# Quantised block and attention in one block of engine programs, with the first batch's adapter, norm and query/key products between the tiles 21 to 31

## The reference

```python
# 1: quantised block, FF = 1024
scale = cond @ norm_w.T + 1.0
h = x * (scale[:, None, :] * rsqrt(mean(x * x, -1) + 1e-6))
val, gate = split(h @ up_w.T)                  # up_w: [2048, 256]
h = val * gelu(gate)
x = act_quant(h) @ weight_quant(down_w).T + x  # 8-bit rows, ternary weights
# 2: adapter whose weights a generator makes for each batch from cond
Wd_b, Wu_b = Wd + 0.1 * (cond @ Wdd.T + bdd), Wu + 0.1 * (cond @ Wdu.T + bdu)
x = x + relu(x @ Wd_b.T + bd) @ Wu_b.T + bu    # bottleneck of 128
# 3: attention, 16 heads of 16, then a gated feed-forward block
a = gamma * rmsnorm(x) + beta
x = x + alpha * (softmax(q @ k.T / 4) @ v) @ W_o.T
x = x + alpha2 * swiglu(gamma2 * rmsnorm(x) + beta2)
# 4: layer norm with weight, bias and tanh(cond @ lin_w.T + lin_b)
```

## Time and profile before

| | us |
|---|---|
| three executions, median | 1230.28 |
| lowest and highest | 1226.63 and 1235.0 |
| the profiled execution | 1235.64 |
| its span, first to last instruction | 1233.8 |
| PE, DVE, ACT, POOL busy in the span | 1078.5, 720.0, 660.9, 220.4 |
| mean granted TensorE clock | 0.92 |

### The profile page before, as it was taken

One profiled execution on the slowest core, in us unless ns is written; L12 is line 12 of the kernel. 1 busy time (PEld: TensorE's weight loads), 2 busy tenths in 40 slices (PEclk: granted clock), 3 DMA queues, 4 the chain that ended last, 5 costly groups with the idle time before them and its releaser, 6 DMA issues. The chain is left out here.

```text
span 1233.8 us, 16846 instructions
## 1 busy us (share of the span) xinstructions
PE 1078.5 (87%) x5282; PEld 648.6 (53%) x5282; DVE 720.0 (58%) x1166; ACT 660.9 (54%) x890; POOL 220.4 (18%) x261
## 2 busy tenths in 40 slices
PE   4879999995569999999999999998629999999994
PEld 3657777773334434443434343333118777777772
DVE  3756666666145767767776777673035455555553
ACT  4463333333214777877776877665333445554445
POOL 0000000001423244544443444311000000000000
PEclk9889999997665999999999999997669999999997
DMA  9622222230152435354545353531030000000000
GB/s 316 233 74 77 78 77 77 78 105 13 39 141 80 122 94 153 103 138 103 145 100 148 89 157 91 159 67 35 11 120 1 1 17 17 17 17 0 17 18 34
DMA packets 63007, 103.66 MB, mean 84 GB/s; under 512 B 18416, under 2 KB 28144, under 8 KB 61936
## 3 DMA queue, kind: packets, MB, share of 16 engines
q1 hardware_dynamic: 60064, 100.43, 28.0%
q10 hardware_dynamic: 2896, 2.64, 0.9%
HBM read 65.81 MB, written 33.03 MB: 80 GB/s over the span
## 5 line engine op out<-in xcount | busy, mean ns | idle before, releaser
L1099 DVE TENSOR_REDUCE mx<-mx_ps 128x1 f32<-128x512 f32 x512 | 329.9, 685 | 176.4 <-PE mx_ps L1154 176.3
L1154 PE MATMUL mx_ps<-kring,qring 48*128 48x512 f32 x512 | 212.5, 484 | 16.5 <-DVE mx L1099 9.3
L1203 PE MATMUL st_ps<-qring,kring 50*128 50x512 f32 x512 | 195.9, 465 | 14.0 <-ACT shared L1032 10.7
L1203 PEld LDWEIGHTS st_ps<-qring,kring 50*128 50x128 f32 x512 | 81.3, 194 | 171.4 <-issue 108.7
L1032 ACT ACTIVATE pbuf<-st_ps 128x1024 f32<-128x1024 f32 x128 | 129.0, 1022 | 47.1 <-PE st_ps L1203 45.3
L1032 ACT ACTIVATE shared<-st_ps 128x1024 f32<-128x1024 f32 x128 | 128.6, 1023 | 38.8 <-PE st_ps L1203 37.7
L1154 PEld LDWEIGHTS mx_ps<-kring,qring 48*128 48x128 f32 x512 | 90.5, 194 | 56.5 <-DVE mx L1099 47.7
L1375 ACT ACTIVATE p_hi<-shared 128x512 fp32r<-128x512 f32 x64 | 40.4, 631 | 93.6 <-DVE shared L1445 93.6
L1449 DVE TENSOR_TENSOR p_lo<-shared,p_hi 128x512 fp32r<-128x512 f32 x64 | 44.3, 692 | 59.2 <-ACT p_hi L1375 59.2
L479 DVE SCALAR_TENSOR_TENSOR h<-val_ps,r,gelu 128x1024 f32<-128x1024 f32 x32 | 41.1, 1284 | 63.7 <-PE val_ps L563 63.7
L1193 PE MATMUL av_ps<-pbuf,vaug 128*17 128x512 f32 x512 | 71.9, 640 | 3.0 <-ACT oaug L962 2.8
(11 more groups left out here) (215 smaller groups left out, 2160.9 us busy)
## 6 DMA issues: line engine op xcount, KB each, us to landing
chunk<-in_gen_w SPq DMA_DIRECT2D x8, 2048.0 KB, 7.7
qring<-q_parts SPq DMA_DIRECT2D x64, 192.0 KB, 3.5
kring<-k_parts SPq DMA_DIRECT2D x64, 192.0 KB, 4.5
q_parts<-stage SPq DMA_DIRECT2D x16, 512.0 KB, 2.8
k_parts<-stage SPq DMA_DIRECT2D x16, 512.0 KB, 2.8
xres<-in_xT SPq DMA_DIRECT2D x8, 512.0 KB, 10.4
shared<-in_x SPq DMA_DIRECT2D x8, 512.0 KB, 9.8
q_parts<-stage SPq DMA_DIRECT2D x16, 256.0 KB, 3.0
```

What stands on the lines that cost most here:

```text
L1099: nc.vector.tensor_reduce(mx[h // GH % 2][:, col:col + 1], mx_ps[qt % 2][:], AX, ALU.max).then_inc(S["mx_free"], 1)
L1154: nc.tensor.matmul(mx_ps[qt % 2][:], qring[r:r + QROWS, h // GH, h % GH // 2, qt * P:(qt + 1) * P], kring[r:r + QROWS, h // GH, h % GH // ...
L1203: ins = nc.tensor.matmul(st_ps[half][:, kt % 2], kring[r:r + SROWS, g, i % GH // 2, kt * P:(kt + 1) * P], qring[r:r + SROWS, g, i % GH // ...
```

## The change

Blocks 1 and 2 become one function, `quantised_and_attention`, with one list of instructions per engine and no meeting between them. The body of an attention step becomes a function `step(j, ..., i)` on each engine, and `opening` hands out the steps of the iterations -1 and 0 one after another, up to the point that tables by tile name. From iteration 1 on they are looped as before.

- All 32 tiles are written out. The generator makes one round in each of the tiles 2 to 17 (`round_of`), stored by ACT one tile later; SP reads `gen` back once after the last, and DVE adds the base in the tiles 20 to 27. SP loads the attention weights after tile 8's residuals, ACT makes their high parts in tiles 18 and 19, and POOL (before: DVE) the low parts.
- The steps of batch 0 stand in the tiles 21 to 31: adapter down product after down(20) in tile 22, up products at the ends of tiles 22 and 23, mean product in tile 25, query/key products in tiles 27 to 30, stores of the parts by SP as they come. The table of ACT's functions is switched in tile 25 for Ln and Exp and back for the next Gelu.
- After tile 31: down(30), the value products, the transposes of q(31) and x1(30), steps up to (0, 9) with the first head's maxima, down(31), its transposes, then steps up to (0, 15).
- A query/key part goes otherwise from PSUM to `stage`, in every batch: ACT copies the high part straight there, DVE subtracts it from PSUM for the low part, at its place in the step behind the early reductions. The bank is free after that (`qk_lo`). The four products of batch 0 use `misc` too, not the score banks.
- SBUF is laid out by hand: weights and buffers of the opening steps share the place of the generator's chunks, the rings and pbuf share that of the up weights and tile buffers. So the first load of a ring waits for the last value product (`val_done`, NT), and the ones of vaug, the zeros of av_ps and the minus ones in kring are made late: the latter by four DMAs of a row each (`key_units`), queued on SP between ring groups 0 and 1.

```diff
+ACT_PLAN = {21: (-1, 7), 22: (-1, 8), 24: (-1, 11), 25: (-1, 14), 26: (0, 1), 27: (0, 2), 31: (0, 5)}
+DVE_PLAN = {23: (-1, 10), 24: (-1, 11), 28: (0, 2), 29: (0, 3), 30: (0, 4), 31: (0, 5)}
+PE_PLAN = {(22, "gate"): (-1, 8), (22, "val"): (-1, 9), (23, "val"): (-1, 10), (25, "gate"): (-1, 13),
+           (27, "gate"): (0, 1), (28, "val"): (0, 2), (29, "val"): (0, 3), (30, "val"): (0, 4)}
...
+        def opening(step):
+
+            order = [(j, i) for j in (-1, 0) for i in range(NH)]
+            taken = [0]
+
+            def upto(j, i):
+                while taken[0] < len(order) and order[taken[0]] <= (j, i):
+                    step(*flags(order[taken[0]][0]), order[taken[0]][1])
+                    taken[0] += 1
+            return upto
...
+            for cc in range(2, NCHUNK):
+                sp.wait_ge(A["gen_ps"], ROUNDS * (cc - 1))
+                sp.dma_start(chunk[cc % 2][:], gen_w[cc]).then_inc(A[f"chunk{cc % 2}_loaded"], 16)
+                if cc == 4:
+                    sp.wait_ge(A["x1"], 2 * KT)
+                    load_attention_weights(sp)
...
                 if isinstance(b, int) and b == 0:
-                    sp.wait_ge(S["setup"], 2)
+                    sp.wait_ge(A["val_done"], NT)
...
-                        nc.gpsimd.tensor_copy(stage[m % 2][:, 0], tmp[:]).then_inc(S["qk_hi"], 1)
-                        wait_apart(pool, "qk_hi", 4 * p + m + 1, (S["mx_zeroed"], 2))
-                        sub(stage[m % 2][:, 1], tmp[:], stage[m % 2][:, 0].bitcast(F32)).then_inc(S["qk_lo"], 1)
...
-                        copy(tmp[:], qk_bank(j, m)).then_inc(S["qk_f"], 1)
+                    wait(act, f"qk{m % 2}_out", 16 * STORES * (2 * p + m // 2))
+                    copy(stage[m % 2][:, 0], misc[:]).then_inc(S["qk_hi"], 1)
...
+                if 2 <= i < 6 and has_p:
+                    m = i - 2
+
+                    wait(dve, "qk_hi", 4 * p + m + 1)
+                    nc.vector.tensor_tensor(stage[m % 2][:, 1], misc[:], stage[m % 2][:, 0].bitcast(F32),
+                                            ALU.subtract).then_inc(S["qk_lo"], 1)
...
-                            take_misc("qk_f", 4 * p + m + 1)
+                    take_misc("qk_lo", 4 * p + m + 1)
...
+                        if (n, "gate") in PE_PLAN:
+                            upto(*PE_PLAN[n, "gate"])
...
+                        if (n, "val") in PE_PLAN:
+                            upto(*PE_PLAN[n, "val"])
+            down(NT - 2)
+            upto(0, 6)
+            transpose_q(NT - 1)
+            transpose_x1(NT - 2)
+            upto(0, 9)
+            down(NT - 1)
+            transpose_x1(NT - 1)
+            upto(0, NH - 1)
```

1556 lines of the change are left out of this document (789 added, 767 removed).

## The result

| | before | after |
|---|---|---|
| median, same chip (4 runs each), us | 1231.74 | 1188.76 |
| lowest and highest | 1226.63 to 1235.0 | 1181.76 to 1199.82 |
| the profiled execution, its span | 1235.64, 1233.8 | 1181.76, 1180.0 |
| PE, DVE, ACT, POOL busy | 1078.5, 720.0, 660.9, 220.4 | 1058.6, 730.2, 664.8, 165.9 |

The ratio is 0.9643, with a 95% interval from 0.961 to 0.9677: 43 us faster; 34 had been forecast (1196.0, range 1182 to 1214). A second profile of the changed kernel (run r1_after) has a span of 1187.6. Its steps are read beside the first wherever that matters.

What follows compares the result with a forecast made beforehand. TensorE was taken to bound the quantised stage and nearly the attention loop, but not 286 to 400 us. Regular steps 37.6 us earlier, plus 3.5 for the hand-over, gave -34.1 from 1230.3: 1196 us, range 1182 to 1214.

Steps and rivals of the forecast that it cites:

- Moved products: Tiles 21 to 30: batch 0's adapter, mean and query/key products lengthen the tiles by their TensorE time, +10.85 us.
- stalls: Tiles: TensorE waiting on the moved steps' work on other engines, +1.5 us, bounds 0 and 22.
- Rival B: Tiles stall: GpSimd blocks DVE on the shared port, 8 us (1204), or chains cost 22 us (1216); chance 0.2.
- The new tail: From T, the transposes' start after tile 31's value product, to the first maximum product: 13.5 us, between 12.4 and 16.5 (half clock).
- rival A: Clock stays full through tail, maxima and first regular steps, worth 10 us, giving 1186; chance 0.18.
- rival D: After tile 31: ring comes no earlier, waiting for late key parts; up to 10 us more, 1206; chance 0.07.
- Maxima: Before the regular steps: first head and up-adapter product 4.3 us, down(31) with transposes 3.15, six heads 22.6; together 30.0.
- The hand-over: Attention loop: DVE's subtraction after ACT's copy delays the fourth maximum product 0.5 us in each of 7 batches, +3.5 us.
- Rival C: Query/key steps: reductions and maxima stand still 1.9 us in each of 28 steps, loop +53 us, 1246; chance 0.03.
- The sum: Whole kernel: regular steps begin 37.6 us earlier, hand-over adds 3.5, total -34.1 us, median 1196.

Runs made afterwards that it cites:

- r1_after: The changed kernel itself, unmodified, timed and profiled again beside the first group of follow-ups; 1188.51 us, ratio to the kernel before 0.967.
- r1_pool_split: Changed kernel with the old hand-over of query/key parts: ACT copies to tmp, POOL casts and subtracts; 1189.35 us, ratio to before 0.9665.
- r3_end_zero: Changed kernel with av_ps cleared earlier and unused matmuls at the loop's end, two a step in j = 8, up to nine in j = 9; 1178.86 us.
- r2_warm_end: Changed kernel with unused matmuls at the loop's end, four a step in j = 8 from i = 9, ten in j = 9; 1193.07 us.

## Why the prediction was right, and where its terms were off

The mechanism was the one foreseen, the chain of batch 0 taken out of the stretch where nothing else runs, paid for in TensorE's time in the tiles. By its steps:

1. **Moved products, forecast +10.85, and stalls, +1.5; measured +7.9 together.** From the starts of the gate products, and beside a tile without a moved product or a generator round (7.11 us), tile 22 is longer by 2.14 us, 23 by 0.69, 25 by 0.86 and 27 to 30 by 1.36 to 1.48 each, 9.3 in all. The other tiles give back 1.3 of it, 1.0 already at the start of tile 2 (44.93 instead of 45.92), where the opening of the kernel changed. No product in tiles 21 to 30 waits, so the stalls were none. The mis-sized term is the price of a product: I had taken 1.59 us for six matmuls from a step of the loop, and in the tiles it costs 1.4. The 1.59 holds wider steps from and to the score products (its first and last matmul take 0.34 and 0.32 us to the next start); in the tiles the product joins a stream of its own kind, in which matmuls start every 0.23 us, and 6 x 0.23 is 1.4. The nearer row was the tile's own.
2. **Rival B, the port that DVE and POOL share.** The mechanism is there, and it was the gaps that saved the tiles. DVE's rounding and its quantised q take 0.75 and 0.69 us when POOL is idle. Four of them, all in tiles 22 to 31, started while POOL was in an operation, and took 1.07, 1.23, 0.88 and 2.76 us. The first and the longest, each with POOL's subtraction (timelines of DVE and of POOL):

```profile
217.15 1.07 DVE L1024 TENSOR_SCALAR rnd<-h,asc 128x1024 f32<-128x1024 f32 x1
289.62 2.76 DVE L1030 TENSOR_SCALAR q<-rnd 128x1024 bf16<-128x1024 f32 x1
```

```profile
215.26 2.40 POOL L515 TENSOR_TENSOR m_lo<-xres,m_hi 128x1024 fp32r<-128x1024 f32 x1
289.38 2.45 POOL L515 TENSOR_TENSOR m_lo<-xres,m_hi 128x1024 fp32r<-128x1024 f32 x1 [32.72 <-ACT m_hi L674]
```

POOL's operations ended at 217.66, 249.86, 256.66 and 291.83, and DVE's 0.55 to 0.56 us after each: whatever was left of POOL's operation (0.51, 0.68, 0.33 and 2.21 us), DVE was done only after it. The Trainium skill (SBUF — State Buffer, on the port pair of DVE and GpSimd) says that the later of the two blocks until the other's instruction is done; the trace agrees, with 2.07 us lost of the 2.21 that were left in the longest case. The product h (1.28 us at 214.00) and the row maximum (1.22 at 215.32) beside POOL took their usual time, so not every operation of DVE pays. In all DVE lost 3.0 us in four places, not the 8 us beyond its idle time that rival B had. In most tiles it had 0.69 to 2.69 us of idle time ahead of h to take that; in tile 26 it had none (h at 253.19 starts right behind the residual, after a loss of 0.47 us at 249.18). TensorE saw nothing; whether it would have with the longest loss in that tile no run shows. ACT in tiles 25 and 26 was as tight as written: two table loads and no idle time from 243.5 to 255 us, with the gelu at 249.75 in time.
3. **The new tail, forecast 13.5, measured 11.1.** Down(30) began at T + 1.7 as worked out, but the second value product at T + 5.2 where I had it start at T + 5.8, and the adapter product at T + 9.5 instead of T + 10.8: rows that follow one another overlap (ACT's three copies, 1.02, 0.38 and 0.60 long, take 1.78 from the first start to the last end), and I had added their full lengths and hand-overs. I had gone from 12.4 up to 13.5 for fear of the half clock; it came 8 us after the first maximum product, so for the tail rival A was right. It came with no idle stretch over 1.65 us ahead of it; that none reaches 4 us, the prediction's reason for a fuller clock, didn't keep it up. The ring was never late (rival D): the first load was issued at 296.77.
4. **Maxima, forecast 30.0, measured 29.6, partly by luck.** The first head and the adapter product took 3.7 us instead of 4.3 and down(31) with its transposes 2.0 instead of 3.15, both at full clock, which the rows of before were not. The other six heads took 22.5 instead of 22.6, nearly all at half clock, as forecast. That would be 28.2; the other 1.42 us are the wait for the clearing of `av_ps`, which the text of the change named as made late and I didn't put on the path.
5. **The hand-over, forecast +3.5: not there.** The medians of r1_pool_split and r1_after are 0.8 apart, but their intervals alone would let 3.5 us pass. The stretches of the loop above speak against it: 473.1 to 476.0 us with the new hand-over in eleven of twelve profiles, 476.4 and 480.9 with the old. Per batch the four query/key steps do cost about 1 us more (from the first product's start to the fourth's 12.16 us before, 511.23 to 523.39, and 13.16 after, 465.53 to 478.69). That shorter waits for the reciprocals and steps that ACT sets the pace of give it back fits the waits shown; how much each gives is not measured. Rival C, 1.9 us a step, didn't appear.
6. **The sum, and what it leaves open.** +12.35 became +7.9, 13.5 became 11.1, 30.0 became 29.6: the first score product came 7.2 us ahead of the forecast. The median did so too (1188.8 instead of 1196), but the terms missed by more: with the 3.5 us of the hand-over they add up to 10.7. The other 3.5 us are not located. The forecast subtracted a saving read from one profiled execution, which lay 4 us above its median, from a median; that execution took 50.4 us from j = 8 to j = 9, more than any other, and the scatter of this stretch is a term that the prediction didn't have and that isn't the change's.

## What to carry to other kernels

A chain of small dependent steps that stands alone between two dense stages is worth its whole length; moved into the dense stage it costs only its TensorE time, and that is to be priced from a row of the stage where it goes. Matmuls without a use can hold TensorE's clock, but their number decides: two a step at the loop's end came with a stretch 5 us below the middle of the others, four and ten a step with one 4 us above it, and four behind each maximum product cost 19 us. Those put into a long wait gained nothing that the traces show. Look for such a gain in the place where it should arise, not only in the median. When executions of one kernel scatter, compare the granted clock and the long waits of two profiles before explaining it by the change. And an engine's idle time covers a collision only tile by tile: here it was 0.69 to 2.69 us in most and nothing in one.

## What the hardware showed that I had not expected

The granted clock fell to half in a stretch in which TensorE counted as busy for 19.19 of 20 us, its matmuls starting 0.3 to 0.4 us apart, and stayed full where four in a row followed each of them. The busy time of the profile doesn't tell the two apart; the distance from start to start does in these two runs. In r3_end_zero two added matmuls a step were enough, in another stretch. What exactly the chip looks at isn't settled by these runs.

The clock can also fall in the middle of the loop, in one execution and not in another. The profiled execution of r2_warm_end (1202.54 us, the slowest of its six; the others lie between 1191.6 and 1197.2) ran at half rate from 390 to 420 us, where its program is that of the changed kernel; there r1_after kept 1.00. The windows of the one and of the other:

```profile
390.00:400.00 10.00, 10.00 (x38) 3.21 (x34) 5.24 (x9) 4.51 (x5) 0.46 (x2) 0.50 0.20 36
400.00:410.00 10.00, 10.00 (x40) 3.12 (x32) 5.28 (x9) 5.75 (x9) 2.50 (x2) 0.50 0.21 47
410.00:420.00 10.00, 10.00 (x34) 4.37 (x30) 4.08 (x7) 5.91 (x8) 4.87 (x7) 0.51 0.26 49
```

```profile
390.00:400.00 10.00, 9.18 (x52) 3.09 (x50) 7.86 (x14) 7.26 (x10) 2.97 (x4) 1.00 0.08 15
400.00:410.00 10.00, 9.12 (x52) 3.25 (x50) 7.17 (x14) 8.90 (x13) 5.28 (x8) 1.00 0.47 95
```

Both had waited 0.78 and 0.79 us for ACT's copy of the weighted values just before, so what made the clock fall in the one isn't shown. The output product of j = 2 came 122.1 us after the first score product there and 110.2 in r1_after, 12 us for one dip. The changed kernel's two executions of 1199.82 and 1200.58, 11 and 12 us above its median, would fit such a dip; they weren't profiled.
